# A transformer layer on one core: the keys of cross-attention's second head group, the ones rows, residual sums and weight splits at other places of the order

## The reference, cut to what matters

```python
x = layernorm(tgt, ln1)                          # (8, 224, 512)
q, k, v = heads(x @ sa_wqkv)                     # self-attention, causal
wei = softmax(mask(q @ k.T * C ** -0.5))
result = tgt + merge(wei @ v) @ sa_wproj + sa_bproj
xq, xs = layernorm(result, ln2), layernorm(src, ln2)   # src: (8, 750, 512)
k2, v2 = heads(xs @ ed_wkv);  q2 = heads(xq @ ed_wq)
wei2 = softmax(q2 @ k2.T * C ** -0.5)            # cross-attention, (16, 224, 750) a sequence
result = result + merge(wei2 @ v2) @ ed_wproj + ed_bproj
h = relu(layernorm(tgt, ln3) @ ff_w1 + ff_b1)
return result + h @ ff_w2 + ff_b2
```

## Time and profile before

| what | us |
|---|---|
| median of three runs | 1375.05 |
| profiled execution | 1375.4 |
| its span, first to last instruction | 1372.8 |
| PE busy in it | 1305.6 (95%) |
| DVE, ACT, POOL busy | 792.8, 665.2, 703.2 |
| mean granted TensorE clock | 0.986 |

### The profile page before, as it was taken

The page is one execution under the profiler, slowest core; times in us unless marked ns, Lnnn a source line. Parts: engine busy times, 40 slices in busy tenths (PEclk is TensorE's granted clock), DMA queues, the critical chain, the costliest instruction groups (busy, mean ns, idle before and its releaser), DMA issues.

```text
span 1372.8 us, 24596 instructions
## 1 busy us (share of the span) xinstructions
PE 1305.6 (95%) x9193; PEld 1081.4 (79%) x9193; DVE 792.8 (58%) x2003; ACT 665.2 (48%) x1611; POOL 703.2 (51%) x581
## 2 busy tenths in 40 slices
PE   7999999999899899999887999999999999999997
PEld 6888888888788788888666777878878787887874
DVE  6613223232776678776635575755757566575565
ACT  5311111232765666555613656474565747456444
POOL 3232221332445455549441757666676756667661
PEclk9999999999999999999899999999999999999999
DMA  7400102124655576578347685777677587767551
GB/s 240 144 17 16 62 31 77 46 60 117 153 150 161 171 197 175 143 165 258 95 90 136 95 133 100 129 117 133 101 121 125 107 137 103 140 99 117 86 75 41
DMA packets 102128, 160.06 MB, mean 117 GB/s; under 512 B 10389, under 2 KB 63421, under 8 KB 100730
## 3 DMA queue, kind: packets, MB, share of 16 engines
q1 hardware_dynamic: 102010, 158.50, 54.8%
HBM read 70.93 MB, written 28.31 MB: 72 GB/s over the span
## 4 chain that ended last, share of the span: by engine, by line
PE 77%; POOL 8%; issue 5%; DVE 4%; DMA 4%; ACT 2%; SPq 1%; POOLq 0%; ACTq 0%; DVEq 0%
PE ps L1747 19%; PE ps L453 11%; PE ps L164 10%; PE ps L423 10%; PE ps_pair L1764 6%; PE ps L1779 5%; PE ps L1793 5%; PE ps L1856 3%; DMA ca_k_stack<-ca_keys 2%; POOL ca_partial L1609 2%; POOL ca_xT L1496 2%; PE ps L1226 1%; PE ps L1811 1%; POOL sa_rows L157 1%; POOL sa_fin L1045 1%
## 5 line engine op out<-in xcount | busy, mean ns | idle before, releaser
L1686 DVE TENSOR_REDUCE ca_maxes<-ps 112x1 f32<-112x375 f32 x512 | 256.7, 540 | 117.2 <-PE ps L1779 115.2
L1630 ACT ACTIVATE ca_probT<-ps_pair 125x448 f32<-125x448 f32 x384 | 210.6, 555 | 181.3 <-PE ps_pair L1764 179.4
L1609 POOL TENSOR_TENSOR ca_partial<-ca_partial,ca_probT 125x896 f32<-125x896 f32 x118 | 249.6, 2115 | 93.3 <-ACT ca_probT L1630 88.6
L312 POOL TENSOR_TENSOR ff_hT<-ff_hrelu,ff_hT 128x512 fp32r<-128x512 f32 (+1 forms) x64 | 78.9, 1235 | 203.3 <-DVE ff_hT L394 203.3
L1779 PE MATMUL ps<-ca_k_stack,ca_q_stack 96*112 96x376 f32 x512 | 168.2, 352 | 13.7 <-issue 11.5
L1764 PEld LDWEIGHTS ps_pair<-ca_q_stack,ca_k_stack 98*125 98x125 f32 x768 | 130.3, 186 | 44.0 <-issue 31.9
L1747 PE MATMUL ps<-ca_xT,w_a 128*128 128x376 f32 x768 | 157.2, 342 | 2.6 <-POOL ca_xT L1496 2.3
L1764 PE MATMUL ps_pair<-ca_q_stack,ca_k_stack 98*125 98x224 f32 x768 | 156.2, 285 | 1.3 <-ACT ca_probT L1630 1.1
L423 PE MATMUL ps<-ff_w,ff_hT 128*128 128x512 f32 x672 | 155.5, 390 | 0.0
L1747 PE MATMUL ps<-w_b,ca_xT 128*125 128x512 f32 x576 | 150.8, 398 | 2.5 <-POOL ca_xT L1496 2.5
L423 PEld LDWEIGHTS ps<-ff_w,ff_hT 128*128 128x128 f32 x672 | 125.6, 188 | 25.7
...
## 6 DMA issues: line engine op xcount, KB each, us to landing
...
```

The source lines that it names most:

```text
L312: pool.tensor_tensor(hT[:, LO, m % RING, 0:width(g)], hrelu[i % 2][:, 0:width(g)], hT[:, HI, m % RING, 0:width(g)].bitcast(F32), ALU.subtr ...
L1609: pool.tensor_tensor(total, total, half(a), ALU.add).then_inc(partial_done, 1)
L1630: act.activation(probT[u // GH][0:JT, u % GH].rearrange("p a t -> p (a t)"), ps_p[u % 2][0:JT, 0:2 * T], ACT.Exp).then_inc(exp_done, 1)
L1686: dve.tensor_reduce(maxes[:, q, j, a:a + 1], ps_s[n % 3][0:TQ, 0:JH], AX_X, ALU.max).then_inc(s_read, 1)
```

## The change

Five things move; no arithmetic is added or left out.

1. EARLY: both halves of K(1) are made right behind the last P products, ahead of V(0), V(1) and V(2); their transfers and those of q_stack go with them. The transfers of K(0) wait for the last self-attention score instead of for the value products; the first q_stack load waits for the value products, not for the outputs.
2. `stack_ones` is two memsets of 2 x 6016 instead of one of 2 x 12032. The first stands behind the last inverse root, the second behind the split of the last Y.
3. `finish` of the last two sequences comes five slots behind P instead of one, and POOL's T_rest items stand one place earlier.
4. Weight pieces 2 to 5 are rounded in slots 45, 61, 77 and 93 instead of 41, 53, 65 and 77, the two reorderings come in slots 51 and 67 instead of 45 and 57.
5. The first context's rows are measured and normalised one to four slots later.

```diff
-NEXT_CONTEXT = [(-2, 6), (-3, 10), (-3, 11)]
-NEXT_MEASURED = {0: (2,), 1: (3,), 2: (4,), 3: (5,), 9: (0,), 10: (1,)}
+NEXT_CONTEXT = [(-2, 6), (-2, 2), (-2, 3)]
+NEXT_MEASURED = {4: (2,), 5: (3,), 6: (4,), 7: (5,), 11: (0,), 12: (1,)}
-NEXT_NORMALISED = {11: (0,), 13: (1,), 15: (2,), 17: (3,), 19: (4,), 21: (5,)}
+NEXT_NORMALISED = {13: (0,), 15: (1,), 17: (2,), 18: (3,), 19: (4,), 20: (5,)}
 EARLY = {
...
-    (5, BEHIND): values_of(0),
+    (5, BEHIND): keys_of(1, 0),
+    (6, BEFORE): scores_of(0, 2),
...
-PREPARED_WEIGHTS = [12, 24, 36, 48, 60, 72]
+PREPARED_WEIGHTS = [(12, 17), (24, 29), (36, 45), (54, 61), (70, 77), (86, 93)]
+TURN = 6
+FINISHED_LATE, STORED_LATE = 5, 12
...
-            rest += [("variance", b), ("finish", b)]
+            rest.append(("variance", b))
...
+            if (name, m) == ("P", 1):
+                rests[n + (FINISHED_LATE if c >= B - 2 else 1)].append(("finish", c))
...
+            elif u - 1 in BY_HEADS:
+                sp.wait_ge(wo_turned, BY_HEADS.index(u - 1) + 1)
...
+            if u - 1 in BY_HEADS:
+                act.wait_ge(wo_stored, 32 * u)
...
             if G == 0:
+                sa.wait(sp, "value_products")
+            if G == 1:
                 sa.wait(sp, "outputs", "scaled")
...
             if G == 0:
+                sa.wait(sp, "scores")
+            if G == 2:
                 sa.wait(sp, "value_products", "maxima")
...
         if name == "stack_ones":
-            sa.wait(pool, "maxima", "value_products", "split_before_ones")
-            pool.memset(k_stack[KS:KM].bitcast(F32), 1.0).then_inc(constants_ready, 1)
-            pool.wait_ge(constants_ready, 2)
+            half = item[1]
+            sa.wait(pool, "maxima", "value_products", ("last_root", "last_split")[half])
+            pool.memset(k_stack[KS:KM, H // 2 * half:H // 2 * (half + 1)].bitcast(F32), 1.0).then_inc(constants_ready, 1)
+            pool.wait_ge(constants_ready, 2 + half)
```

More of the change, by code:

```diff
@@ L615 @@
     (-11, BEFORE): [turned(0, 0)],
-    (-10, BEFORE): [turned_rest(0, 0), turned(1, 0)],
-    (-9, BEFORE): [turned_rest(1, 0), turned(2, 0)],
-    (-8, BEFORE): [turned_rest(2, 0), turned(3, 0)],
-    (-7, BEFORE): [turned_rest(3, 0), turned(0, 1)],
-    (-6, BEFORE): [turned_rest(0, 1), turned(1, 1)],
-    (-6, BEHIND): [("K", 0, 0, 0)],
-    (-5, BEFORE): [turned_rest(1, 1), turned(2, 1), ("context", 1, 0)],
-    (-5, BEHIND): [("K", 0, 0, 1)],
-    (-4, BEFORE): [("K_rest", 0, 0), turned_rest(2, 1), turned(3, 1)],
@@ L625 @@
-    (-3, BEFORE): [turned_rest(3, 1), ("context", 1, 1)],
+    (-11, BEHIND): [turned_rest(0, 0)],
+    (-10, BEFORE): [turned(1, 0)],
+    (-10, BEHIND): [turned_rest(1, 0)],
+    (-9, BEFORE): [turned(2, 0)],
+    (-9, BEHIND): [turned_rest(2, 0)],
+    (-8, BEFORE): [turned(3, 0)],
+    (-8, BEHIND): [turned_rest(3, 0)],
+    (-7, BEFORE): [turned(0, 1)],
+    (-7, BEHIND): [turned_rest(0, 1)],
+    (-6, BEFORE): [turned(1, 1)],
+    (-6, BEHIND): [turned_rest(1, 1), ("K", 0, 0, 0)],
+    (-5, BEFORE): [turned(2, 1)],
@@ L626 @@
+    (-5, BEHIND): [turned_rest(2, 1), ("context", 1, 0), ("K", 0, 0, 1)],
+    (-4, BEFORE): [("K_rest", 0, 0), turned(3, 1)],
+    (-4, BEHIND): [turned_rest(3, 1)],
+    (-3, BEFORE): [("context", 1, 1)],
     (-2, BEFORE): keys_of(0, 1),
     (-1, BEHIND): [("K_rest", 0, 1)],
-    (2, BEHIND): [("stack_ones",)],
-    (5, BEHIND): values_of(0),
-    (6, BEHIND): [("queries", 0), *values_of(1)],
-    (7, BEHIND): [*scores_of(0, 2), ("V", 0, 2, 0)],
-    (8, BEHIND): [*scores_of(2, 4), ("V", 0, 2, 1)],
@@ L633 @@
-    (11, BEFORE): [*scores_of(4, 6), *keys_of(1, 0), ("K_rest", 1, 0)],
-    (11, BEHIND): keys_of(1, 1),
-    (12, BEFORE): [("K_rest", 1, 1), ("queries", 1), *scores_of(6, 8)],
-    (13, BEFORE): scores_of(8, 10),
-    (14, BEFORE): scores_of(10, 12),
-    (14, BEHIND): scores_of(12, 14),
-    (15, BEHIND): [*scores_of(14, 16), ("ones",), ("weights",)],
+    (2, BEHIND): [("queries", 0)],
+    (5, BEHIND): keys_of(1, 0),
+    (6, BEFORE): scores_of(0, 2),
+    (6, BEHIND): [("K_rest", 1, 0), *keys_of(1, 1)],
@@ new lines @@
+    (7, BEFORE): scores_of(2, 4),
+    (7, BEHIND): [("K_rest", 1, 1), ("queries", 1), *values_of(0)],
+    (8, BEFORE): scores_of(4, 6),
+    (8, BEHIND): [("stack_ones", 0), *values_of(1)],
+    (9, BEFORE): scores_of(6, 8),
+    (9, BEHIND): values_of(2),
+    (10, BEHIND): scores_of(8, 9),
+    (11, BEHIND): scores_of(9, 10),
+    (12, BEFORE): scores_of(10, 12),
+    (13, BEFORE): scores_of(12, 14),
+    (14, BEFORE): scores_of(14, 16),
+    (15, BEHIND): [("stack_ones", 1), ("ones",), ("weights",)],
@@ L762, in plan_self_attention @@
         items += [("normalise", b - 1, t) for t in range(2) if i == normalised[t] and 0 <= b - 1 < B]
-        if i == 11 and 0 <= b - 1 < B:
+        if i == (STORED_LATE if b == B - 1 else 11) and 0 <= b - 1 < B:
             items.append(("store", b - 1))
@@ L768, in plan_self_attention @@
             rests[n + 1].append(("keep_y", u))
-        for u, first in enumerate(PREPARED_WEIGHTS):
-            if n == first:
+        for u, (loaded, split) in enumerate(PREPARED_WEIGHTS):
+            if n == loaded:
                 items.append(("load_prepared", u))
-            if n == first + 5:
+            if n == split:
                 items.append(("round_prepared", u))
                 rests[n + 1].append(("keep_prepared", u))
-            if n == first + 9 and u in BY_HEADS:
+            if n == split + TURN and u in BY_HEADS:
                 items.append(("turn_prepared", u))
@@ L1282, in self_attention @@
                      "key_weights": (next_landed[0], 32), "value_weights": (next_landed[1], 32),
-                     "split_before_ones": (tile_read[tile["Y", B - 2, 1][0]], tile["Y", B - 2, 1][1] + 1),
+                     "scores": (s_psum, H * B),
+                     "last_root": (ln2.rstd_done, B),
+                     "last_split": (tile_read[tile["Y", B - 1, KT - 1][0]], tile["Y", B - 1, KT - 1][1] + 1),
                      "last_tile_read": (tile_read[TILES - 1], 1 + max(n for i, n in tile.values() if i == TILES - 1)),
```

4 lines of the change are left out of this document (2 added, 2 removed).

## The result

The changed kernel takes 1359.62 us (median of four runs, 1358.47 to 1362.29) against 1375.14 us (four runs, 1374.71 to 1375.65): a ratio of 0.989, with a 95% interval of 0.9873 to 0.9907. That is 15.5 us faster; 1357.3 was forecast, with a range of 1350 to 1364.

A forecast was written before the change was run, and what follows sets the result against it. PE, busy 1305.6 of 1372.8 us, was taken as the bound, leaving its idle time and lower-clock losses to win. Terms 5.2 + 3.0 + 11.5 - 2.0 = 17.7 us gave a median of 1357.3 us, range 1350 to 1364.

The forecast's parts named there:

- The boundary up to step 2: From P's end to step 2: earlier key transfers remove waits of 5.89 and 3.58 us; gain 11.5, bounds 8 and 12.8.
- Step 2: Step 2 of cross-attention: second memset delays the key issue and the lower clock follows; costs 2.0 us more.
- The hold: In step 2, DVE's small TENSOR_SCALAR falls inside POOL's second memset, holding the issue of K(2) some 2.4 us.
- Weight pieces: Third and fourth self-attention sequences: later split and reordering avoid ACT's store stall; gain 5.2 us, bounds 3.5 and 7.3.
- rival B: Reorderings at slots 51 and 67 still wait for their store, 6.9 us each; 1369.5 us, chance 0.12.
- Piece 5 moves into a sequence that is relieved of some context work: nothing.: Later split of weight piece 5 in self-attention: claimed to cost nothing, as that sequence loses some context work.
- Context rows and residual sums: Up to the end of P: PE's waits of 0.65 and 2.31 us for POOL go; gain 3.0, bounds 1.5 and 4.5.
- A: Step 2: the second memset holds nobody, so the step wins 1.9 us instead of losing 2.0; 1353.4 us, chance 0.13.
- C: Boundary: first scores still wait as queries and keys share the engines, 4 us in all; 1361.3 us, chance 0.14.
- D: PE stays at the lower clock through the boundary, costing 24.8 us; 1382 us, slower than before, chance 0.03.
- E: Waits move but the end stays, because step 3 gives back cross-attention's slack; 1372 us, chance 0.03.

The follow-up runs named there:

- b_old: The changed kernel with the boundary's old order of keys, queries, scores and ones (one memset) and old transfer waits; 1369.77 us, ratio 0.9964.
- ctx_old: pieces_early with the loading, measuring and normalising of the context's first rows also back in their old slots; 1361.68 us, ratio 0.9898.
- ones_late: The changed kernel with the second memset of ones moved behind the root of the context's variance and the offset made from it; 1355.89 us, ratio 0.986.
- pieces_early: The changed kernel with weight pieces split at the old slots 41, 53, 65 and 77, reordered 6 slots behind (47 and 59); 1357.06 us, ratio 0.9874.

## Why the prediction was right, and where its terms were not

*The boundary up to step 2.* Right in its mechanism: a wait of 1.4 for Y was forecast and 1.59 measured, and `b_old` puts the gain on the order. That the size is right too (26.2 us forecast, 26.43 measured) is partly luck. "About 681.8" for K(0)'s transfers was 675.33, 6.5 us earlier, 5.2 of them because all of P came earlier. What the term left out is the clock behind the new wait: in the nine kernels with this order and this wait the stretch took from 26.4 us (after, the lowest) to 30.8 (`ctx_old`), 28.0 in the middle, mostly by the rate of the Y products.

*Step 2.* The hold was forecast as it came: the issue 6.4 us behind the step's start (6.66 measured), a TENSOR_SCALAR that ends with the memset. `ones_late` gives 2.3 us for it. The wait at step 3's scores was 2.15 and not 4, because the step could not use the rest: the hold had already stopped PE for 2.48 in the middle of it. 19.83 us against a forecast of 19.05 + 0.5, and the lower clock fell behind step 3's start (0.72 over 6.19 us, 1.7 us lost), where 1.5 was counted. Together -0.8 and -1.7, against -2.0. The Trainium skill, GPSIMD Engine Reference, section Key points, has GpSimd contend with VectorE's two-port instructions for their shared SBUF interfaces; the hold is in the trace, 2.72 against 0.17 us, but in which mode the held operation ran the trace doesn't show.

*Weight pieces.* This term failed. The step was "I put 42.9 for the sequence (42.1, plus 0.5, plus 0.3 for the reordering)": it took the split at slot 45 as costing what a mean sequence pays. It cost more, in both sequences: 43.59 and 43.55 us, 3.4 us gained instead of 5.2. A second reading was wrong, in rival B. It takes all of the 6.9 us of the earlier trace rows as the price of the stall: 1.9 of them were the waits behind the split in slot 41, and in `pieces_early`, without a stall, the split alone took 3.3. The lower bound was also added up wrong. Two sequences at 43.7 make 5.25 - 2.11 = 3.1 us and not 3.5, so the 3.4 measured is outside the bound as written and inside it as reckoned.

*"Piece 5 moves into a sequence that is relieved of some context work: nothing."* Wrong, and it is the mechanism that the forecast missed. The load of four of the six groups of context rows waits until the last piece is stored, since both use the same tile. With piece 5 split at slot 93 its stores stand in SP's queue at 588.22, and the load of the rows follows at 594.68, 25.75 us behind the sequence's start; in `pieces_early` it is issued 23.09 us behind it (592.19) and nobody waits. In after SP has no gap in front of the load, so it is the 2.2 us of issuing the two stores that come late there; in `ones_late` SP stands 2.4 us in front of it (until 596.11), which is the wait for them. DVE stood 2.60 us in front of the rows, with PE's transposed probabilities behind it. The sixth sequence lost 2.1 us against before in the profiled execution and nothing in `ones_late`. Five kernels with the late split take 42.71 to 45.19 us for it, and the six with the early one and the new context slots 41.30 to 41.50. So the new context slots were worth 1.1 us here, and the late split took that back and up to 2.5 more. The chain was in the diff and not in any row of before.

*Context rows and residual sums.* 3.0 forecast, 5.1 measured, above the bound of 4.5. The waits of 0.65 and 2.31 went as forecast. The size was off because the keys behind the wait of 2.31 ran at half rate in before, 2.22 us for six and 2.14 for the next six, and at 1.30 and 1.27 after (before, then after):

```profile
668.32 2.14 PE L1747 MATMUL ps<-ca_xT,w_a 128*128 128x376 f32 x6
```

```profile
660.24 1.30 PE L1772 MATMUL ps<-ca_xT,w_a 128*128 128x376 f32 x6 [0.43 <-ACT ca_xT_f L1698]
...
662.50 1.27 PE L1772 MATMUL ps<-ca_xT,w_a 128*128 128x376 f32 x6
```

The granted clock over the stretch rose from 0.91 to 0.98, and PE's busy time fell from 69.82 to 66.78 us, 3.0 of the 5.1. The forecast counted the clock behind the waits of the boundary and not behind this one. It also put the late load of the last residual at nothing, which cost PE 0.54 us. Sum and low rests undone one by one give 2.8 and 0.4 us; no run undid both, so 1.9 of the 5.1 us are assigned to neither.

*The rivals.* A was excluded by the trace and by `ones_late`. B did not occur (no ACT wait for a store); C neither: no wait at the first scores. D in its strong form did not occur; E neither: from step 3 to the end the kernels take 623.2 to 625.8 us (more only in the two with the moved load), and what is given back is clock: PE is busy 2.85 us longer there with the same matmuls, 1.7 of it in step 3. The total is nearer than its terms. In the profile 13.2 us were gained and 17.7 forecast. Too much was counted for the weights (1.8), the fifth and sixth sequence (1.9), the boundary (0.2), step 2 and all behind it (1.3) and the first stretch (1.4), too little for the stretch up to P (2.1). The medians show 15.5 us, since the profiled execution took 2.7 us more than the median.

*Not settled:* why the clock falls behind the same wait of 1.59 us in seven kernels and not in two, and how much of a median's difference under 2 us is that.
